# A graph layer with routed experts: identity transposes put ahead of TensorE's waits in the routing stage, behind the feed-forward and ahead of the experts' products

## The chip, the cores and the metric

The kernel runs on one core of one Trainium2 chip. A core has a matrix engine (TensorE, PE in the profile; its weight loads are listed as PEld), a vector engine (DVE), a scalar engine (ACT), GpSimd (POOL) and SyncE (SP). Each runs its own stream of instructions in order and waits for the others through semaphores. Sixteen DMA engines move data between the chip's memory and SBUF. The metric is the device time of one execution in microseconds, the median of the runs. The profile's rows show TensorE at one of two levels: the granted clock is 1.00 (2.4 GHz) or 0.50 (1.2 GHz).

## The reference

Everything is fp32. `x` has 6250 rows of 256. A graph attention layer (106250 edges) with batch normalisation comes first, its last part being a feed-forward of two 256x256 products over all nodes. Then each row is normalised, routed to the two best of eight experts, and the two experts' outputs are added to it:

```python
h = _batchnorm(x_attn + x, gamma1, beta1)
ffn = relu(h @ W1 + b1) @ W2 + b2
x = x + _batchnorm(ffn + h, gamma2, beta2)
z = _layernorm(x)
gate_scores = z @ Wg + bg                       # 6250 x 8
_, idx = top_k(gate_scores, 2)
h_e = gelu(z @ W1[e] + b1[e])                   # 256 -> 512, for the two chosen experts
y_e = h_e @ W2[e] + b2[e]                       # 512 -> 256
out = x + sum of y_e over the two chosen
```

## The kernel before

The program is a row of blocks with a barrier of all engines between them: preparing the edges, projecting the nodes, attention (the first two thirds of the time), joining the heads, the feed-forward, the routing, the experts, and a copy of the result. All of it is written out by hand, with semaphores. Three blocks are touched.

**Feed-forward** (`feed_forward`, L1367). The nodes go through in chunks of 250 columns. For each chunk TensorE does `up` (L1454) and `down` (L1463), eight instructions each. After the last `down` (L1475) TensorE has nothing left in this block, while VectorE finishes sums and the batch scale.

**Routing** (`route_tokens`, L1478). 6250 rows are 49 tiles of 128, in eight groups of 3, 5, 6, 7, 7, 7, 7, 7 tiles. For a tile t:

- ScalarE writes the batch-normalised features `y` (L1590, two per tile, semaphore `y_ready`), in a ring of three.
- TensorE turns them with two 128x128 transposes into `y_ps` (`turn_y`, L1639, semaphore `y_turned`).
- VectorE adds them to the rows of x (L1717, `summed`) and measures them (L1722). For a whole group it forms the row scale (`spread`, `inverse`), with a root on ScalarE.
- ScalarE writes the normalised rows `z` (L1607, `z_ready`); TensorE turns them with two transposes (`turn_z`, L1647); ScalarE copies them out of PSUM (L1597, `z_taken`); TensorE multiplies them with the 256x8 gate weights (`score`, L1660, four instructions of 8 columns, `scored`).
- VectorE chooses the experts of the group (12 small operations), TensorE counts ranks with four small matmuls (`ranks`, L1671 and L1672), VectorE turns ranks into places (11 small operations, the last one L1824), and GpSimd scatters each tile's rows twice, once for each chosen expert (L1892, indirect DMAs).

TensorE's order in group g is, for i = 0 to 7: `turn_y` of tile i of group g+1, `turn_z` of tile i of group g, `score` of tile i-1 of group g; `ranks` of group g-1 stands in the middle of the loop. VectorE interleaves `choose` and `places` of one group with the sums of a later one.

**Experts** (`apply_experts`, L1897). 56 slots of 256 rows. A slot has four transposes (`turn_z`, L1973), 16 instructions of `up` (L1982) and 16 of `down` (L1992). Ahead of the loop TensorE turns the biases (L1998), waits for the rows of slots 0 and 1 (`loaded`), turns them, and does `up(0)`; the loop begins with `up(1)`.

Of the kernel before, what the change touches and what calls it, by code (L numbers as in the profile page):

```python
# [16 lines left out]
P = 128  # L17
# [52 lines left out]
CHUNKS = N // W  # L70
# [48 lines left out]
def wait_past(engine, semaphore, value):  # L119

    if isinstance(value, int) and value <= 0:
        return
    engine.wait_ge(semaphore, value)
# [8 lines left out]

class Program:
    pass


def heads_of(row):
# [1229 lines left out]
def feed_forward(nc, k):  # L1367


    with ExitStack() as ctx:  # L1370
# [7 lines left out]
        up_ps = pb("f_up_ps", [P, 2, 2, 256])  # L1378
        down_ps = pb("f_down_ps", [P, 2, 2, 256])
        w_in = k.ffn_in  # L1380
        normed, up_done, hid_ready, down_done, summed, measured = (sem("f_normed"), sem("f_up"), sem("f_hid_s"), sem("f_down"),
                                                                   sem("f_summed"), sem("f_measured"))

        with nc.Block(no_gpsimd_drain=True) as block:
# [62 lines left out]
            @block.tensor  # L1447
            def _(pe):
                def up(c, s):
                    pe.wait_ge(normed, 2 * c + 2)  # L1450
                    wait_past(pe, hid_ready, 2 * c - 2)
                    for o in range(DH):
                        for h in range(DH):
                            last = nc.tensor.matmul(up_ps[:, s, o, 0:W], w1[:, h, o * P:(o + 1) * P],  # L1454
                                                    k.feat[:, h, bass.ds(c * W, W)], start=(h == 0), stop=(h == DH - 1))
                    last.then_inc(up_done, 1)

                def down(c, s):
                    pe.wait_ge(hid_ready, 2 * c + 2)
                    wait_past(pe, summed, 2 * c - 2)  # L1460
                    for o in range(DH):
                        for h in range(DH):
                            last = nc.tensor.matmul(down_ps[:, s, o, 0:W], w2[:, h, o * P:(o + 1) * P], hid[:, s, h],  # L1463
                                                    start=(h == 0), stop=(h == DH - 1))
                    last.then_inc(down_done, 1)

                pe.wait_ge(w_in, 96)
                up(0, 0)

                def both(c, s):  # L1470
                    up(c + 1, 1 - s)
                    down(c, s)

                tiles(pe, CHUNKS - 1, 2, 2, both)
                down(CHUNKS - 1, (CHUNKS - 1) % 2)  # L1475


def route_tokens(nc, k):  # L1478
# [6 lines left out]
    CHOICE, STEPS = 12, 22  # L1485
    half_of = lambda g: GROUPS[g] // 2
    Y_RING = 3
    tokens = lambda t: min(P, N - t * P)
    tiles_of = lambda g: range(FIRST[g], FIRST[g + 1]) if 0 <= g < len(GROUPS) else ()
    with ExitStack() as ctx:  # L1490
# [14 lines left out]

        y = spare((Y_RING, DH, P))
        zt = spare((2, DH, P))
# [33 lines left out]
        slot_f = sb("r_slot_f", [1, 2, SLOT_STEPS])  # L1541
        y_ps = pb("r_y_ps", [P, Y_RING, 512])
        zt_ps = pb("r_zt_ps", [P, 2, 512])
# [4 lines left out]
        y_ready, y_turned, summed, measured = sem("r_y_s"), sem("r_y_turned"), sem("r_summed"), sem("r_measured")  # L1548
        z_ready, z_turned, z_taken, scored = sem("r_z_s"), sem("r_z_turned"), sem("r_z_taken"), sem("r_scored")
# [4 lines left out]
        with nc.Block(no_gpsimd_drain=True) as block:  # L1554
# [30 lines left out]
            def _(act):  # L1585
                def norm(t):
                    n = tokens(t)
                    wait_past(act, y_turned, t - (Y_RING - 1))
                    for h in range(DH):
                        nc.scalar.activation(y[:, t % Y_RING, h, 0:n], k.feat[:, h, t * P:t * P + n], ACT.Identity,  # L1590
                                             scale=k.norm2[:, 0, h:h + 1], bias=k.norm2[:, 1, h:h + 1]).then_inc(y_ready, 1)
# [40 lines left out]
            @block.tensor  # L1632
            def _(pe):
                def turn_y(t):
                    n = tokens(t)
                    pe.wait_ge(y_ready, 2 * t + 2)
                    wait_past(pe, summed, t - (Y_RING - 1))
                    for h in range(DH):
                        last = nc.tensor.transpose(y_ps[0:n, t % Y_RING, h * P:(h + 1) * P], y[:, t % Y_RING, h, 0:n], k.ident[:, :])  # L1639
                    last.then_inc(y_turned, 1)  # L1640

                def turn_z(t):
                    n = tokens(t)
                    pe.wait_ge(z_ready, t + 1)
                    wait_past(pe, z_taken, t - 1)
                    for h in range(DH):
                        last = nc.tensor.transpose(zt_ps[:, t % 2, h * P:h * P + n], z[0:n, t, h * P:(h + 1) * P], k.ident[0:n, 0:n])  # L1647
                    last.then_inc(z_turned, 1)

                def biases(g):  # L1650

                    n = GROUPS[g]
                    nc.tensor.matmul(score_ps[:, g % 2, 0:n * E], ones[0:1, :], bg_all[:, 0:n, :].rearrange("o t e -> o (t e)"),
                                     start=True, stop=False, skip_group_check=True)

                def score(g, t):
                    n, i = tokens(t), t - FIRST[g]
                    pe.wait_ge(z_taken, t + 1)
                    for h in range(DH):
                        last = nc.tensor.matmul(score_ps[0:n, g % 2, i * E:(i + 1) * E], zt[:, t % 2, h, 0:n], wg[:, h, :],  # L1660
                                                start=False, stop=(h == DH - 1), skip_group_check=True)
                    last.then_inc(scored, 1)

                def ranks(g):
                    pe.wait_ge(routed, g * STEPS + CHOICE)
                    flat = either[:, :, :].rearrange("p t e -> p (t e)")
                    n = GROUPS[g]
                    whole = n if tokens(FIRST[g + 1] - 1) == P else n - 1
                    spans = [(0, whole, P)] + [(whole, n, tokens(FIRST[g] + whole))] * (whole < n)
                    for a, b, m in spans:  # L1670
                        nc.tensor.matmul(rank_ps[:, 0, a * E:b * E], below[0:m, :], flat[0:m, a * E:b * E], start=True, stop=True)  # L1671
                        last = nc.tensor.matmul(rank_ps[:, 1, a * E:b * E], ones[0:m, :], flat[0:m, a * E:b * E], start=True, stop=True)  # L1672
                    last.then_inc(ranked, 1)

                for t in tiles_of(0):
                    turn_y(t)
                pe.wait_ge(w_in, before_route + 32)
                pe.wait_ge(biased, 1)
                for g in range(len(GROUPS)):
                    biases(g)  # L1680
                    if g == 1:
                        ranks(0)
                    for i in range(G + 1):
                        if i < len(tiles_of(g + 1)):
                            turn_y(tiles_of(g + 1)[i])
                        if i < len(tiles_of(g)):
                            turn_z(tiles_of(g)[i])
                        if 1 <= i <= len(tiles_of(g)):
                            score(g, tiles_of(g)[i - 1])
                        if 2 <= g < LAST and i == half_of(g + 1):  # L1690
                            ranks(g - 1)
                ranks(LAST - 1)
                ranks(LAST)
# [203 lines left out]
def apply_experts(nc, k):  # L1897

    RING = 4
    with ExitStack() as ctx:  # L1900
# [21 lines left out]
        zt_ps = pb("x_zt_ps", [P, 2, DH, BATCH])  # L1922
        hid_ps = pb("x_hid_ps", [P, 2, HC, BATCH])
        y_ps = pb("x_y_ps", [P, 2, 2, D])
# [10 lines left out]
        with nc.Block(no_gpsimd_drain=True) as block:  # L1935
# [31 lines left out]
            def _(pe):  # L1967
                def turn_z(s, q):
                    pe.wait_ge(loaded[q % RING], (s - q % RING) * (32 // RING) + 32)
                    wait_past(pe, zt_ready, s - 1)  # L1970
                    for h in range(DH):
                        for u in range(2):
                            last = nc.tensor.transpose(zt_ps[:, q % 2, h, u * P:(u + 1) * P],  # L1973
                                                       z[:, q % RING, u, h * P:(h + 1) * P], k.ident[:, :])
                    last.then_inc(z_turned, 1)
# [11 lines left out]
                def down(s, q, e):  # L1987
                    pe.wait_ge(hid_ready, HC * s + HC)
                    wait_past(pe, y_ready, s - 1)
                    for u in range(2):  # L1990
                        for j in range(HC):
# [5 lines left out]
                pe.wait_ge(k.bias_in, 16 * (E + 1))  # L1997
                nc.tensor.transpose(y_ps[:, 0, 0, 0:E * HC], k.be1_rows[:, :],  # L1998
                                    k.ident[0:E * HC, 0:E * HC]).then_inc(bias_turned, 1)
                turn_z(0, 0)  # L2000
                turn_z(1, 1)
                pe.wait_ge(k.experts_in, 16 * E)
# [9 lines left out]
                n = SLOT_STEPS - 2  # L2012
# [77 lines left out]
def graph_ffn_kernel(nc, *args):  # L2090
# [23 lines left out]
    with ExitStack() as ctx:  # L2114
# [59 lines left out]
        with ExitStack() as layer:  # L2174
# [3 lines left out]
            join_heads(nc, k)  # L2178
            feed_forward(nc, k)
        route_tokens(nc, k)  # L2180
        apply_experts(nc, k)
        give_out(nc, k)
# [16 lines left out]
```

## Time and profile before

| | us |
|---|---|
| median of 3 runs | 2530.99 (2528.05 to 2534.24) |
| the profiled execution, its span | 2534.7 (the execution: 2536.48) |
| feed-forward, TensorE's part | about 1773 to 1861 |
| routing, TensorE's part | about 1867 to 2041 |
| wait for the last scatters and the barrier | about 2041 to 2079 |
| experts | about 2079 to the end |

Times inside the execution are counted from the start of the span. In a row of the profile "MATMUL a<-b,c x4" means four instructions on PE that write tile a; the time behind it reaches from the first's start to the last's end, or is the sum of busy time in a view of groups. A transpose on TensorE is listed as a MATMUL with `ident` among its inputs. Ends of matmuls are modelled.

### The profile page before, as it was taken

The numbers are of one execution on the slowest core, as the hardware profiler recorded it, in microseconds if no ns is written. First come the engines' busy times: TensorE is split into PE (matmuls) and PEld (weight loads), VectorE is DVE, ScalarE is ACT, GpSimd is POOL, SyncE is SP. The second block draws the span as 40 slices with busy tenths as digits, with TensorE's granted clock in tenths as the row PEclk, the third lists the DMA queues.
The fourth block names the chain that finished last, engine by engine and source line by source line (L and its number), as shares of the span: only waits on it lengthen the run. The fifth ranks groups of instructions, "written<-read, shape, count | busy, mean of one in ns | idle before, by whom it ended". The sixth has DMA issues, their size and how long they took to land. (4 is left out here: it accounts for less than half of the span.)

```text
span 2534.7 us, 43098 instructions
## 1 busy us (share of the span) xinstructions
PE 1952.2 (77%) x9344; PEld 1654.9 (65%) x9345; DVE 1530.2 (60%) x3518; ACT 1183.7 (47%) x2733; POOL 1364.5 (54%) x1263
## 2 busy tenths in 40 slices
PE   3974787888788878887888788853966519999994
PEld 2754676676676766776776667732855418888884
DVE  5955777777777777787777777889455311111110
ACT  3542555555555555555555555543545403223221
POOL 3346666666666666666666666538003543444442
PEclk9987998999899989998999899875975559999997
DMA  7676666666666666666666666533503345666665
GB/s 216 230 245 191 185 198 189 187 195 189 188 190 191 190 189 187 188 195 189 190 190 187 191 190 186 153 101 121 165 29 106 127 150 127 142 143 145 139 143 143
DMA packets 259360, 430.75 MB, mean 170 GB/s; under 512 B 46025, under 2 KB 130872, under 8 KB 259180
## 3 DMA queue, kind: packets, MB, share of 16 engines
q1 hardware_dynamic: 156320, 227.87, 28.1%
q0 software_dynamic: 66272, 154.09, 23.7%
q10 hardware_dynamic: 36716, 48.20, 6.1%
q8 instruction: 19, 0.31, 0.0%
q14 instruction: 33, 0.27, 0.0%
HBM read 365.32 MB, written 71.10 MB: 172 GB/s over the span
## 5 line engine op out<-in xcount | busy, mean ns | idle before, releaser
L820 POOL DMA_INDIRECT ring<-xl_rows,a_idx x928 | 956.1, 1030 | 514.6 <-issue 249.7
L1137 PE MATMUL a_f_ps<-a_xr_w,a_hot_n 128*128 128x256 f32 x1856 | 577.9, 393 | 59.2 <-ACT a_hot_n L884 31.1
L1139 PE MATMUL a_f_ps<-ring,ident 128*128 128x256 f32 x1856 | 584.1, 396 | 18.8 <-issue 18.7
L1150 PE MATMUL a_o_ps<-ring,a_hot_e 128*128 128x264 f32 x1856 | 532.6, 412 | 41.9 <-issue 21.0
L1137 PEld LDWEIGHTS a_f_ps<-a_xr_w,a_hot_n 128*128 128x128 f32 x1856 | 372.5, 202 | 132.9 <-issue 36.7
L1004 DVE SCALAR_TENSOR_TENSOR a_pos<-a_f_ps,att_cols 128x512 f32<-128x512 f32 x464 | 316.2, 681 | 224.9 <-remote 155.1
L1150 PEld LDWEIGHTS a_o_ps<-ring,a_hot_e 128*128 128x128 f32 x1856 | 367.0, 204 | 123.3 <-issue 43.9
L901 ACT ACTIVATE a_hot_e<-a_far_e,one 128x512 f32<-128x512 f32 x232 | 167.3, 721 | 352.4 <-PE a_o_ps L1150 168.8
L1014 DVE TENSOR_REDUCE a_lg<-a_pos 128x8 f32<-128x512 f32 x464 | 315.8, 681 | 15.3 <-remote 14.6
L1022 DVE TENSOR_TENSOR ring<-ring (+1 forms) x464 | 316.8, 683 | 7.3 <-ACT ring L929 3.9
L1139 PEld LDWEIGHTS a_f_ps<-ring,ident 128*128 128x128 f32 x1856 | 303.0, 200 | 26.0 <-issue 25.9
L1959 POOL DMA_INDIRECT acc_rows<-ring,x_idx x112 | 175.3, 1566 | 261.0 <-DVE ring L2057 133.5
L894 ACT ACTIVATE a_far_e<-iota_row,a_near_rel 128x128 f32<-128x128 f32 x928 | 294.8, 388 | 1.6 <-issue 0.3
L1034 DVE TENSOR_TENSOR acc<-a_o_ps,acc 128x264 f32 x464 | 197.3, 425 | 125.5 <-PE a_o_ps L1150 59.0
L884 ACT ACTIVATE a_hot_n<-a_far_n,one 128x512 fp32r<-128x512 f32 x232 | 167.5, 722 | 190.7 <-remote 117.2
L2056 DVE CAST x_idx<-ring 128x2 int32<-128x2 f32 x56 | 9.5, 170 | 408.7 <-PE x_y_ps L1992 408.7
L1982 PE MATMUL x_hid_ps<-ring,x_w 128*128 128x256 f32 x896 | 204.5, 382 | 0.0
L1992 PE MATMUL x_y_ps<-we,ring 128*128 x896 | 202.5, 379 | 0.0
L1982 PEld LDWEIGHTS x_hid_ps<-ring,x_w 128*128 128x128 f32 x896 | 171.8, 192 | 23.7
L1992 PEld LDWEIGHTS x_y_ps<-we,ring 128*128 128x128 f32 x896 | 166.0, 190 | 20.3
L878 ACT ACTIVATE a_far_n<-a_rel_bc,neg_col 128x512 f32<-128x512 bf16 x232 | 164.9, 711 | 22.7 <-issue 19.5
L1892 POOL DMA_INDIRECT disp_rows<-r_z,r_idx x98 | 96.7, 987 | 109.7 <-DVE r_idx L1824 82.3
(323 smaller groups left out, 2050.1 us busy)
## 6 DMA issues: line engine op xcount, KB each, us to landing
a_xr_w<-xr_rows SPq DMA_DIRECT2D x464, 256.0 KB
a_rel_bc<-rel_rows ACTq DMA_DIRECT2D x116, 256.0 KB
x_w<-in_L_ffn_W_dram SPq DMA_DIRECT2D x56, 512.0 KB
ring<-xl_rows,a_idx POOLq DMA_INDIRECT x928
ring<-disp_rows SPq DMA_DIRECT2D x56, 257.0 KB
xr_rows<-xr_parts SPq DMA_DIRECT2D x50, 256.0 KB, 2.0
xl_rows<-xl_sb SPq DMA_DIRECT2D x50, 132.0 KB, 1.8
j_xl<-xl_rows SPq DMA_DIRECT2D x25, 264.0 KB, 2.8
```

Source lines behind the costliest of these rows:

```text
L820: nc.gpsimd.indirect_dma_start(xl_e[:, p * T + 2 * h + u, :], None, k.xl_rows, bass.IndirectOffsetOnAxis(ap=idx[:, p, 2 * h + u:2 * h + u ...
L894: nc.scalar.activation(far_e[:, u, :], k.iota_row[:, :], ACT.Abs, bias=near_rel[:, j * QT + u:j * QT + u + 1]).then_inc(far_e_ready, 1)
L1004: nc.vector.scalar_tensor_tensor(pos[:, h % 2], f_ps[:, h % FS], 0.0, att, ALU.max, ALU.mult).then_inc(settled, 1)
L1014: nc.vector.tensor_reduce(lg[:, :, 2 * h:2 * h + 2].rearrange("p h t -> p t h"), pos[:, h % 2].rearrange("p t (h c) -> p t h c", c=C), AX. ...
L1022: nc.vector.tensor_tensor(at[:, :, :, 0:C], at[:, :, :, 0:C], at[:, :, :, C:C + 1].to_broadcast([P, 2, H, C]), ALU.mult).then_inc(msg_read ...
L1034: nc.vector.tensor_tensor(at, o_ps[:, o_slot(hh), 0:XW], at, ALU.add).then_inc(added, 1)
L1137: nc.tensor.matmul(f_ps[:, h % FS, u, :], hot_n[:, j % 2, 2 * g + u, :], xr_w[:, h % XR, a, :].bitcast(F32R), start=(a == 0), stop=False)
L1139: last = nc.tensor.matmul(in_heads(f_ps[:, h % FS, u, :]), k.ident[:, :], heads_of(xl_e[:, p * T + 2 * h + u, :])[:, :, 0:C], start=False, ...
L1150: last = nc.tensor.matmul(o_ps[:, o_slot(hh), 0:XW], hot_e[:, j % 2, 2 * g + u, :], xl_e[:, pp * T + 2 * hh + u, :], start=(u == 0), stop= ...
L1959: nc.gpsimd.indirect_dma_start(k.acc_rows, bass.IndirectOffsetOnAxis(ap=idx[:, q, u:u + 1], axis=0), y[:, q, u], None, compute_op=ALU.add) ...
L1982: last = nc.tensor.matmul(hid_ps[:, q % 2, j], w1[:, q % RING, h, j * P:(j + 1) * P], zt[:, q % 2, h], start=(h == 0), stop=(h == DH - 1))
L1992: last = nc.tensor.matmul(y_ps[:, q % 2, u], hid[:, q % 2, j, u * P:(u + 1) * P], k.we2[:, bass.ds(e, 1), j, :].rearrange("p o n -> p (o n)"),
```

## The change

A helper is added that issues n transposes of the 128x128 identity into a given piece of PSUM. No instruction reads what they write, and they raise no semaphore.

```diff
+def keep_warm(nc, k, out, n):
+    for _ in range(n):
+        nc.tensor.transpose(out, k.ident[:, :], k.ident[:, :])
...
                 tiles(pe, CHUNKS - 1, 2, 2, both)
                 down(CHUNKS - 1, (CHUNKS - 1) % 2)
+                keep_warm(nc, k, up_ps[:, CHUNKS % 2, 0, 0:P], 50)
...
+    FILL = 4
...
                 def turn_y(t):
                     n = tokens(t)
+                    wait_past(pe, summed, t - (Y_RING - 1))
+                    keep_warm(nc, k, y_ps[:, t % Y_RING, 0:P], FILL)
                     pe.wait_ge(y_ready, 2 * t + 2)
-                    wait_past(pe, summed, t - (Y_RING - 1))
...
                 def turn_z(t):
                     n = tokens(t)
+                    wait_past(pe, z_taken, t - 1)
+                    keep_warm(nc, k, zt_ps[:, t % 2, 0:P], FILL)
                     pe.wait_ge(z_ready, t + 1)
-                    wait_past(pe, z_taken, t - 1)
...
                 nc.tensor.transpose(y_ps[:, 0, 0, 0:E * HC], k.be1_rows[:, :],
                                     k.ident[0:E * HC, 0:E * HC]).then_inc(bias_turned, 1)
+                keep_warm(nc, k, hid_ps[:, 0, 0, 0:P], 36)
                 turn_z(0, 0)
```

So there are 50 transposes behind the feed-forward's last product, 2 x 4 for each of the 49 tiles of the routing (392), and 36 ahead of the experts' first rows. In the rows of the changed kernel the helper is L141; other lines of these blocks move down by 7 to 11.

On TensorE, at the border of the feed-forward and the routing. Before:

```order
L1463 MATMUL f_down_ps<-f_hid,f_w 128x250 [waits f_summed,f_hid_s]
L1463 MATMUL f_down_ps<-f_hid,f_w 128x250 x3
L1384 UNCONDITIONAL_BRANCH
L1632 UNCONDITIONAL_BRANCH [waits barrier_Pool_Activation_PE_DVE_SP_release]
L1639 MATMUL r_y_ps<-ident,ring 128x128 [waits r_y_s]
L1639 MATMUL r_y_ps<-ident,ring 128x128
```

And changed:

```order
L1470 MATMUL f_down_ps<-f_hid,f_w 128x250 [waits f_summed,f_hid_s]
L1470 MATMUL f_down_ps<-f_hid,f_w 128x250 x3
L141 MATMUL f_up_ps<-ident 128x128 x50
L1391 UNCONDITIONAL_BRANCH
L1641 UNCONDITIONAL_BRANCH [waits barrier_Pool_Activation_PE_DVE_SP_release]
L141 MATMUL r_y_ps<-ident 128x128 x4
L1649 MATMUL r_y_ps<-ident,ring 128x128 [waits r_y_s]
L1649 MATMUL r_y_ps<-ident,ring 128x128
```

The 50 stand ahead of the barrier, so TensorE reaches it after them; the first four of the routing stand behind it, ahead of the wait for `y` (the semaphore of tile `y` is called r_y_s here).

On TensorE, one tile in the middle of a routing group (a tile of the next group turned, one of this group turned, one scored). Before:

```order
L1639 MATMUL r_y_ps<-ident,ring 128x128 [waits r_summed,r_y_s]
L1639 MATMUL r_y_ps<-ident,ring 128x128
L1647 MATMUL r_zt_ps<-ident,r_z 128x128 [waits r_z_taken,r_z_s]
L1647 MATMUL r_zt_ps<-ident,r_z 128x128
L1660 MATMUL r_score_ps<-r_wg,ring 128x8 [waits r_z_taken]
L1660 MATMUL r_score_ps<-r_wg,ring 128x8
```

And changed:

```order
L141 MATMUL r_y_ps<-ident 128x128 [waits r_summed]
L141 MATMUL r_y_ps<-ident 128x128 x3
L1649 MATMUL r_y_ps<-ident,ring 128x128 [waits r_y_s]
L1649 MATMUL r_y_ps<-ident,ring 128x128
L141 MATMUL r_zt_ps<-ident 128x128 [waits r_z_taken]
L141 MATMUL r_zt_ps<-ident 128x128 x3
L1658 MATMUL r_zt_ps<-ident,r_z 128x128 [waits r_z_s]
L1658 MATMUL r_zt_ps<-ident,r_z 128x128
L1671 MATMUL r_score_ps<-r_wg,ring 128x8 [waits r_z_taken]
L1671 MATMUL r_score_ps<-r_wg,ring 128x8
```

The wait for a free buffer now stands alone, ahead of the four; the wait for the data stands behind them. Nothing stands ahead of the wait of a score. (A score of one tile is four instructions on the chip, two of these rows with two each.)

On TensorE, at the start of the experts. Before:

```order
L1998 MATMUL x_y_ps<-ident,be_rows 128x32 [waits bias_in]
L1973 MATMUL x_zt_ps<-ident,ring 128x128 [waits x_loaded0]
L1973 MATMUL x_zt_ps<-ident,ring 128x128 x3
L1973 MATMUL x_zt_ps<-ident,ring 128x128 [waits x_loaded1]
L1973 MATMUL x_zt_ps<-ident,ring 128x128 x3
L1982 MATMUL x_hid_ps<-ring,x_w 128x256 [waits x_zt,experts_in]
```

And changed:

```order
L2009 MATMUL x_y_ps<-ident,be_rows 128x32 [waits bias_in]
L141 MATMUL x_hid_ps<-ident 128x128 x36
L1984 MATMUL x_zt_ps<-ident,ring 128x128 [waits x_loaded0]
L1984 MATMUL x_zt_ps<-ident,ring 128x128 x3
L1984 MATMUL x_zt_ps<-ident,ring 128x128 [waits x_loaded1]
L1984 MATMUL x_zt_ps<-ident,ring 128x128 x3
L1993 MATMUL x_hid_ps<-ring,x_w 128x256 [waits x_zt,experts_in]
```

The 36 stand between the biases and the wait for the first slot's rows. The other engines' streams are the same but for line numbers.

## Rows read from the trace of the kernel before

**Rows 1.** The page: span, and the clock granted in 40 equal slices.
```profile
span 2534.7 us, 43098 instructions
...
PEclk9987998999899989998999899875975559999997
```

**Rows 2.** Stretches: us, PE busy (x instructions), granted clock, DMA share, GB/s.
```profile
1773.00:1861.00 88.00, 87.59 (x400) 0.96 0.38 121
1861.00:1867.00 6.00, 0.00 (x0) 0.79 0.00 0
1867.00:2041.00 174.00, 104.77 (x444) 0.50 0.29 99
2098.00:2500.00 402.00, 402.00 (x1971) 1.00 0.61 136
```

**Rows 3.** Groups of PE's instructions, 1866 to 2045: busy, mean ns | idle before, releasers.
```profile
L1660 PE MATMUL r_score_ps<-r_wg,ring 128*128 128x8 f32 (+1 forms) x196 | 45.4, 345 | 34.2 <-ACT ring L1597 27.6 <-issue 6.3
L1639 PE MATMUL r_y_ps<-ident,ring 128*128 128x128 f32 (+1 forms) x98 | 32.6, 436 | 19.1 <-ACT ring L1590 19.0
L1647 PE MATMUL r_zt_ps<-ident,r_z 128*128 128x128 f32 (+1 forms) x98 | 31.9, 431 | 12.7 <-ACT r_z L1607 8.0 <-issue 3.2 <-DVE acc L1717 0.6
```

**Rows 4.** PE in order of time: start, us, instructions, [idle before <-releaser].
```profile
1773.22 6.55 PE L1454 MATMUL f_up_ps<-ring,f_w 128*128 128x250 f32 x16 [6.96 <-ACT ring L1425]
...
1891.10 0.69 PE L1647 MATMUL r_zt_ps<-ident,r_z 128*128 128x128 f32 x2 [4.96 <-ACT r_z L1607]
...
2079.38 0.28 PE L1998 MATMUL x_y_ps<-ident,be_rows 32*128 32x32 f32 x1 [38.44 <-PEq L1554]
...
2087.87 1.12 PE L1973 MATMUL x_zt_ps<-ident,ring 128*128 128x128 f32 x4 [1.65 <-DMA ring<-disp_rows]
2088.78 9.26 PE L1982 MATMUL x_hid_ps<-ring,x_w 128*128 128x256 f32 x32
2097.87 0.60 PE L1973 MATMUL x_zt_ps<-ident,ring 128*128 128x128 f32 x4
```

**Rows 5.** PE in order of time, two tiles of group 2: scores follow one another.
```profile
1908.32 0.86 PE L1660 MATMUL r_score_ps<-r_wg,ring 128*128 128x8 f32 x4
...
1909.92 0.86 PE L1660 MATMUL r_score_ps<-r_wg,ring 128*128 128x8 f32 x4
```

**Rows 6.** One stretch of group 2: us, PE busy, granted clock.
```profile
1908.00:1912.00 4.00, 4.00 (x22) 0.50 0.00 0
```

**Rows 7.** A wait of PE in group 3, in order of time.
```profile
1955.12 1.02 PE L1660 MATMUL r_score_ps<-r_wg,ring 128*128 128x8 f32 x4 [5.75 <-ACT ring L1597]
```

**Rows 8.** GpSimd's scatters as a group, then GpSimd and DVE in order of time.
```profile
L1892 POOL DMA_INDIRECT disp_rows<-r_z,r_idx x98 | 96.7, 987 | 109.7 <-DVE r_idx L1824 82.3 <-issue 27.4
...
1977.03 0.97 POOL L1892 DMA_INDIRECT disp_rows<-r_z,r_idx  x1 [0.30 <-issue]
1985.52 0.96 POOL L1892 DMA_INDIRECT disp_rows<-r_z,r_idx  x1 [7.52 <-DVE r_idx L1824]
...
1980.40 0.22 DVE L1797 COPY r_total<-r_rank_ps 128x56 f32<-128x56 f32 x1 [5.63 <-remote]
```

**Rows 9.** Stretches where the clock changes: us, PE busy, granted clock.
```profile
1862.00:1864.00 2.00, 0.00 (x0) 1.00 0.00 0
1864.00:1866.00 2.00, 0.00 (x0) 0.63 0.00 0
...
1778.00:1780.00 2.00, 2.00 (x8) 0.71 1.10 347
...
2092.00:2094.00 2.00, 2.00 (x8) 0.70 0.00 0
```

**Rows 10.** DVE's last operation of the feed-forward, ACT's first of the routing.
```profile
1865.96 0.16 DVE L1199 TENSOR_TENSOR norm<-f_par,f_tmp 128x2 f32<-128x2 f32 x1
...
1866.67 1.65 ACT L1590 ACTIVATE ring<-ring,norm 128x128 f32<-128x128 f32 x4 [1.94 <-PEq L1384]
```

## The prediction, made before the changed kernel ran

> **What bounds the kernel now.** I first read the slices of the page [rows 1]: the granted clock is near full everywhere but in the joining of the heads and in the routing. The table of stretches [rows 2] puts numbers on it. In the routing (1867 to 2041) TensorE is at 0.50 throughout; in the experts (from 2098 on) it is busy all the time at 1.00. So a microsecond won ahead of the experts is won at the end, and one lost is lost, since TensorE has no idle time there to give back.
>
> Then I asked what ends last inside the routing. It is not one engine. The groups of TensorE's instructions [rows 3] show 19.1 us of idle time ahead of `turn_y` (ScalarE's y is late), 12.7 ahead of `turn_z` and 34.2 ahead of the scores. In the early groups, where nothing else interferes, TensorE works without a gap [rows 6] and a tile takes 1909.92 - 1908.32 = 1.60 us [rows 5]: there TensorE sets the pace, with ScalarE and VectorE close to it. In the four later full-length passes (groups 2 to 5) there is another loop: GpSimd scatters a group (one DMA every 1.27 us), and while it does, TensorE's semaphores arrive late, so that all engines stand still for some 5 us (TensorE 5.75 us [rows 7], VectorE 5.63 us for the ranks [rows 8]). The ranks come only after the scatters' end (1977.03 + 0.97 = 1978.0; VectorE takes them at 1980.40), then VectorE needs until about 1985.5 for the places, and the next scatters start at 1985.52 [rows 8]. In this loop TensorE's speed counts only between 1980.4 and 1985.5: three tiles at 1.60 us.
>
> **The price of a transpose.** At half clock four take 1.12 us and two take 0.69 [rows 4], so one more costs (1.12 - 0.69) / 2 = 0.215 us; at full clock half of that, 0.107 (four: 0.60 [rows 4]). A tile of the routing gets eight more: +1.72 us at half clock, so 1.60 becomes 3.32; at full clock old and new work together take 3.32 / 2 = 1.66. All 392 cost 84.3 us of TensorE at half clock, 42.1 at full. The waits behind them hide at most 19.1 + 12.7 = 31.8 us [rows 3]; the 34.2 ahead of the scores have no transposes ahead of them. So the question is the clock, not the number.
>
> **When the clock moves.** It falls 3.5 us after TensorE has stopped: nothing runs from 1861, and the share 0.63 between 1864 and 1866 puts the fall at 1864.5 [rows 2, 9]. It rises after 5.9 us (1773.22 to 1779.2) and 4.4 us (2088.8 to 2093.2) of products back to back [rows 4, 9]. But in 1908 to 1912 TensorE was busy without a gap and the clock stayed at 0.50 [rows 6]. There half of the instructions are scores with 8 columns and half are transposes. The trace has no long stretch of transposes alone, so it doesn't show whether they raise the clock. With the change 12 of a tile's 16 instructions are transposes of 128 columns. I take it that they do count, since they stream the same columns through the array as a product does and follow one another at the same pace at either level; nothing in the trace says so directly.
>
> The Trainium skill says otherwise: "TensorE: Matmul & The Clock Gate", Part 4 (PE-mode transpose), states that the full clock does not engage for transposes, as they don't count as busy in the same way. By that rule the change would only add work. The same place gives 390 ns alone and 275 ns inside a kernel for one transpose.
>
> **Part 1, behind the feed-forward.** At full clock 50 x 0.107 = 5.3 us from 1860.9 on, to 1866.2. VectorE ends its part at 1866.1 and ScalarE starts the routing at 1866.67 [rows 10]; the cover is just long enough: 0 to +0.4, I take +0.2. If the clock falls at 1864.5 all the same, 34 are done and 16 x 0.215 = 3.4 us remain, to 1867.9: +1.7.
>
> **Part 2, the routing.** The clock starts high, but in groups 0 and 1 TensorE waits 4.96 us at a time for z [rows 4], with only four or eight transposes ahead of the wait, so it falls. From then on each working stretch starts at half clock and rises after 4.4 to 5.9 us: 1.3 to 1.8 tiles at 3.32 instead of 1.60, +2.3 to +3.1, say +2.7. For the stretch at 1891 all of this is on the path: +2.7. After each of the four standstills in the later passes it is so too, but the transposes ahead of the first turns have run during the standstill; I take half, 4 x 1.35 = +5.4 (bounds 0 and 4 x 3.1 = 12.4). At the high level a turn and a score end sooner (four transposes 1.12 against 0.60 [rows 4], so two win about 0.25 and a score about 0.4), which shortens the way from the row scale to the first score and the ranks: about -0.65 in five groups, -3.2 (bounds 0 and -6.5). Sum of the routing: +2.7 + 5.4 - 3.2 = +4.9, bounds -4 and +15. The buffer waits that now come first are on the same semaphores as before, and nothing else is queued behind them than what was: 0.
>
> **Part 3, ahead of the experts.** The biases are turned at 2079.4 to 2079.7; the rows of slot 1 arrive at 2087.87 [rows 4]. 36 transposes take 36 x 0.215 = 7.7 us at half clock, to 2087.4, inside that wait. If the clock rises meanwhile they end near 2086, and the 1.9 us to 2087.87 are shorter than the 3.5 us after which it fell. Then `up` of slots 0 and 1 runs at full clock: now the 4.6 us up to 2093.2 are at half, so -2.3, and -0.2 for the turn of slot 1: -2.5. If nothing rises: 2087.4 + 1.1 for slot 0's turn pushes slot 1's back: 0 to +0.7.
>
> **Sum.** 0.2 + 4.9 - 2.5 = +2.6 on an execution of 2536.5 (span 2534.7 and 1.8 around it). The median is 5.5 lower, so 2531.0 + 2.6, rounded to 2534.
>
> **Rivals.**
>
> A. Transposes don't raise the clock. Then every tile costs 3.32 where TensorE sets the pace. In the early stretches (1891 to 1900, 1903 to 1916) that is 5 + 6 tiles: 11 x 1.72 = +18.9. In each of four later passes 0 to 3 tiles stand on the path between the late semaphores and the next scatters; I take 1.8, as part of the work still runs in the standstill: 4 x 1.8 x 1.72 = +12.4. Bounds 19 and 40, sum +31. With +1.7 and +0.4 of the other parts: +33, 2564. For it: at 1908 to 1912 a gapless mix with transposes stayed low [rows 6]. Against it: there were as many short instructions in it. The rule of the Trainium skill above would give this.
>
> B. They do count, and the clock hardly falls in the routing at all, because the four ahead of each turn bridge the waits. Then 1.66 against 1.60 us costs nothing that the waits don't hide, and the shorter ways win 8 x 0.8 = -6; with -2.5: -8.5, 2522. For it: most waits are under 3.5 us. Against it: those of 5 us.
>
> C. They count, but with scores between them the mix is too thin to raise the clock in most stretches (slower, one mechanism): the early 11 tiles mostly at 3.32, +15, the later passes +7, the ends -2.5: about +20, 2551. It decides from the point where a tile's four scores keep the clock from rising.
>
> **How the numbers follow.** Likeliest case 47% (own range 2525 to 2543), A 25% (2552 to 2573), B 18% (2516 to 2526), C 10%. What a measurement can tell from no change is 0.2%, 5 us. Faster by more: B and the low end of the likeliest (0.07): 0.25. Within: most of the likeliest, 0.28. Slower by more: A, C and the high end (0.12): 0.47. The range that leaves out 2 in 10 cuts half of B and the upper end of A: 2522 to 2568.
>
> **What would show it.** The granted clock from 1867 on: 0.50 throughout means A; 1.00 throughout means B; a change of level in each group means the forecast, and with it a TensorE that after each standstill takes 3.3 us for the first tile and 1.7 for the third. In the experts the clock should be high by 2088, and the 32 instructions of the first two `up` take 7 us instead of 9.26. The prediction is wrong if the standstills of about 5 us themselves change, which I left as they are, or if other engines than I assume set the pace of the early tiles.

## The result and the profile after

The changed kernel takes 2550.43 us (median of four runs, 2547.33 to 2552.35) against 2530.82 (2528.05 to 2534.24): the ratio is 1.007, 95% interval 1.0056 to 1.0084. That is +19.6 us where the likeliest case said +2.6. The range held it, but by luck: it was wide because it also covered rivals A and B, and the case that I called likeliest (2525 to 2543) did not hold the time. The profiled execution has a span of 2547.5 us, 12.8 more than before; the two executions stand 5.7 above and 1.1 below their medians, so the traces show some 7 us less than the medians do.

First the page of the changed kernel, then three stretches of it (columns: us, busy time and instructions of PE, PEld, DVE, ACT and POOL, granted clock, DMA share, GB/s).

```profile
span 2547.5 us, 43961 instructions
...
PEclk9987988999899989998898989865987759999997
```

```profile
1776.00:1864.00 88.00, 87.56 (x440) 78.96 (x439) 41.01 (x112) 40.62 (x92) 0.18 (x1) 1.00 0.32 100
1864.00:2057.00 193.00, 129.32 (x836) 121.03 (x834) 89.19 (x399) 80.75 (x204) 73.55 (x76) 0.74 0.27 90
...
2110.00:2500.00 390.00, 390.00 (x1913) 343.57 (x1912) 42.95 (x106) 114.93 (x266) 165.44 (x106) 1.00 0.63 139
```

The routing (second stretch) now has a mean clock of 0.74 where [rows 2] had 0.50: about half of it runs at full clock. The stretch is also 19 us longer as cut here; from its first to its last mark the routing grew by 16.8 (table below). In the experts nothing has changed but the beginning. The groups of TensorE's instructions in the routing:

```profile
L141 PE MATMUL r_zt_ps<-ident 128*128 128x128 f32 x196 | 38.4, 332 | 0.0
L141 PE MATMUL r_y_ps<-ident 128*128 128x128 f32 x196 | 37.3, 322 | 0.4 <-PEq L1391 0.4
L1671 PE MATMUL r_score_ps<-r_wg,ring 128*128 128x8 f32 (+1 forms) x196 | 32.6, 276 | 33.8 <-ACT ring L1606 31.1 <-issue 2.2
L1658 PE MATMUL r_zt_ps<-ident,r_z 128*128 128x128 f32 (+1 forms) x98 | 24.6, 342 | 7.3 <-ACT r_z L1616 3.8 <-issue 3.3
L1649 PE MATMUL r_y_ps<-ident,ring 128*128 128x128 f32 (+1 forms) x98 | 22.5, 317 | 10.8 <-ACT ring L1599 10.8
```

Against [rows 3] the waits ahead of `turn_y` and `turn_z` shrank from 19.1 and 12.7 us to 10.8 and 7.3, so the added transposes filled a part of them. The 34.2 us ahead of the scores, where the long waits are, stayed (33.8). The clock goes up and down, here while groups 0 and 1 are scored:

```profile
1872.00:1875.00 3.00, 3.00 (x16) 3.00 (x16) 0.76 (x2) 3.00 (x9) 0.00 (x0) 0.50 0.03 5
1876.00:1881.00 5.00, 2.90 (x27) 2.61 (x24) 3.54 (x14) 1.94 (x5) 0.00 (x0) 1.00 0.21 72
1882.00:1891.00 9.00, 5.55 (x25) 5.15 (x26) 4.81 (x27) 3.17 (x9) 3.50 (x4) 0.50 0.12 41
1893.00:1902.00 9.00, 6.97 (x61) 6.42 (x60) 5.25 (x22) 3.57 (x10) 0.97 (x1) 1.00 0.31 109
```

**Where the time went.** The clearest mark is the start of VectorE's last operation of a group's places (`CAST r_idx`), after which GpSimd can scatter the group. I call the time between two of them a pass and use it for every kernel below. The last row of the table counts from ScalarE's first `y` of the routing to the last group's places.

| us | before | after | e2 | e5 | e6 | e7 | e8 |
|---|---|---|---|---|---|---|---|
| places of group 0 to 1 | 28.6 | 30.1 | 31.3 | 29.3 | 31.1 | 31.3 | 38.7 |
| 1 to 2 | 20.1 | 24.5 | 25.0 | 22.4 | 21.1 | 20.7 | 27.8 |
| 2 to 3 | 22.9 | 26.6 | 27.3 | 24.6 | 24.0 | 23.5 | 30.0 |
| 3 to 4 | 25.1 | 27.7 | 27.7 | 26.6 | 25.1 | 25.2 | 34.9 |
| 4 to 5 | 25.1 | 27.5 | 27.5 | 26.7 | 25.1 | 25.1 | 34.3 |
| 5 to 6 | 25.8 | 27.2 | 28.7 | 28.6 | 25.8 | 25.8 | 32.5 |
| whole | 176.8 | 193.6 | 197.2 | 188.7 | 181.4 | 181.8 | 231.7 |

The routing is 16.8 us longer, and every pass takes part. The four passes from 1 to 2 up to 4 to 5 each hold one standstill ahead of the places that end them; the first pass holds none, and in the last one (5 to 6) no `ranks` stands in the middle of TensorE's loop. (The kernels e1, e3 and e4, whose routing does the same work as before, give 175.2 to 176.2, so such a sum repeats within 1.6 us.)

**Inside a later pass.** TensorE in group 4, first in the kernel before:

```profile
1969.74 0.65 PE L1671 MATMUL r_rank_ps<-r_either,r_below 128*128 128x56 f32 x2
...
1970.62 0.65 PE L1639 MATMUL r_y_ps<-ident,ring 128*128 128x128 f32 x2
...
1976.54 1.02 PE L1660 MATMUL r_score_ps<-r_wg,ring 128*128 128x8 f32 x4 [4.85 <-ACT ring L1597]
...
1980.91 1.03 PE L1660 MATMUL r_score_ps<-r_wg,ring 128*128 128x8 f32 x4 [2.40 <-ACT ring L1597]
```

and in the changed kernel:

```profile
1976.68 0.60 PE L141 MATMUL r_zt_ps<-ident 128*128 128x128 f32 x4
1977.11 0.38 PE L1658 MATMUL r_zt_ps<-ident,r_z 128*128 128x128 f32 x2
1985.44 1.02 PE L1671 MATMUL r_score_ps<-r_wg,ring 128*128 128x8 f32 x4 [7.94 <-ACT ring L1606]
1986.31 0.66 PE L1682 MATMUL r_rank_ps<-r_either,r_below 128*128 128x56 f32 x2
...
1987.18 1.07 PE L141 MATMUL r_y_ps<-ident 128*128 128x128 f32 x4
```

Before, `ranks` and one more tile of y are through when the standstill begins; only the message is late (VectorE takes the ranks at 1980.40 [rows 8]). Now the standstill catches TensorE one tile sooner, with `ranks` still to be done. It isn't much longer: before, TensorE waits 4.85 us, gets one tile further and waits 2.40 more, 7.25 together; now it waits 7.94 at once. What VectorE and GpSimd make of it (for a wait marked `<-remote` the profile names no engine):

```profile
1987.92 0.42 DVE L1728 TENSOR_TENSOR acc<-r_y_ps,acc 128x256 f32<-128x256 f32 x1 [7.00 <-remote]
...
1988.60 0.20 DVE L1808 COPY r_total<-r_rank_ps 128x56 f32<-128x56 f32 x1
...
1991.67 0.42 DVE L1728 TENSOR_TENSOR acc<-r_y_ps,acc 128x256 f32<-128x256 f32 x1 [1.26 <-PE r_y_ps L1649]
...
1995.52 0.97 POOL L1903 DMA_INDIRECT disp_rows<-r_z,r_idx  x1 [10.11 <-DVE r_idx L1835]
```

From the end of the standstill to the next scatter it is 1995.52 - 1987.92 = 7.6 us, where [rows 8] give 1985.52 - 1980.40 = 5.1: VectorE has one more addition to do ahead of the ranks, and then waits for a `turn_y` behind transposes. This is the +2.5 of such a pass.

The pass from group 1 to 2 has the same standstill and loses in the same way. VectorE before, then in the changed kernel:

```profile
1931.06 0.42 DVE L1717 TENSOR_TENSOR acc<-r_y_ps,acc 128x256 f32<-128x256 f32 x1 [5.16 <-remote]
...
1931.90 0.21 DVE L1797 COPY r_total<-r_rank_ps 128x48 f32<-128x48 f32 x1
```

```profile
1931.07 0.42 DVE L1728 TENSOR_TENSOR acc<-r_y_ps,acc 128x256 f32<-128x256 f32 x1 [2.85 <-remote]
...
1933.35 0.21 DVE L1808 COPY r_total<-r_rank_ps 128x48 f32<-128x48 f32 x1 [1.51 <-PE r_rank_ps L1683]
```

The ranks lay ready before; now VectorE waits for TensorE to compute them. From the end of VectorE's last late wait to the places it takes 1940.19 - 1931.07 = 9.1 us against 1936.57 - 1931.06 = 5.5. For groups 3, 4 and 5 the same time is 8.4, 6.6 and 6.4 us against 4.6, 4.1 and 4.1. These four together are +12.2 of the 16.8 us.

**The experts' beginning** in the changed kernel, in order of time, and under it two stretches in which TensorE runs nothing but the added transposes:

```profile
2093.91 5.60 PE L141 MATMUL x_hid_ps<-ident 128*128 128x128 f32 x36
2099.41 0.66 PE L1984 MATMUL x_zt_ps<-ident,ring 128*128 128x128 f32 x4
2101.95 0.66 PE L1984 MATMUL x_zt_ps<-ident,ring 128*128 128x128 f32 x4 [1.88 <-DMA ring<-disp_rows]
2102.44 7.07 PE L1993 MATMUL x_hid_ps<-ring,x_w 128*128 128x256 f32 x32
```

```profile
2094.00:2096.00 2.00, 2.00 (x10) 2.00 (x11) 0.00 (x0) 0.19 (x1) 0.00 (x0) 0.50 0.00 0
2097.00:2099.00 2.00, 2.00 (x20) 2.00 (x19) 0.00 (x0) 0.00 (x0) 0.00 (x0) 1.00 1.00 347
```

The clock rises while only identity transposes run, 10 instructions in 2 us become 20, and the first two `up` take 7.07 us where [rows 4] had 9.26. The DMA share goes from 0.00 to 1.00 between the two stretches as well, but the clock doesn't need that: in [rows 9] it is 0.70, on its way up, in 2092 to 2094 with a DMA share of 0.00.

### The profile page after: what moved, and what is told of

Its sections match the earlier page's. It is cut to its first block and busy times, and to the rows that moved or that the text cites. A ratio compares the mean times of both kernels' runs of the same rounds, so it can differ in the third digit from the quotient of the medians.

```text
span 2547.5 us, 43961 instructions
## 1 busy us (share of the span) xinstructions
PE 1993.6 (78%) x9822; PEld 1702.5 (67%) x9823; DVE 1529.8 (60%) x3518; ACT 1187.2 (47%) x2733; POOL 1368.5 (54%) x1263
## 5 line engine op out<-in xcount | busy, mean ns | idle before, releaser
L1144 PE MATMUL a_f_ps<-a_xr_w,a_hot_n 128*128 128x256 f32 x1856 | 581.3, 395 | 59.7 <-ACT a_hot_n L891 30.1
```

Source lines behind the costliest of these rows:

```text
L1144: nc.tensor.matmul(f_ps[:, h % FS, u, :], hot_n[:, j % 2, 2 * g + u, :], xr_w[:, h % XR, a, :].bitcast(F32R), start=(a == 0), stop=False)
```

## The experiments

The first eight ran on chips where the kernel before takes what it took above (2532.0 and 2532.6 us); the last four on a chip where it takes 2263.1 us, which matters below. Their lines move by up to 11 against the kernel before.

**e1: the 36 ahead of the experts alone.**

```diff
+                keep_warm(nc, k, hid_ps[:, 0, 0, 0:P], 36)
                 turn_z(0, 0)
```

> The kernel before with the 36 transposes ahead of the experts' rows and nothing else. Theory: they hide behind the wait for the rows of slot 1 and raise the clock before `up` of slot 0. In the changed kernel the stretch from the bias turn to the end was 453.8 us against 455.3, so -1.5 us (2529.3), and the granted clock reads 1.00 when `up` of slot 0 starts. Rival: identity transposes by themselves don't raise the clock, and in the changed kernel it was high for another reason: then 0 to +0.7 us, and 32 instructions of `up` take 9.3 us as before.

Measured: ratio 0.9998 (0.9986 to 1.0009), so nothing that the medians can tell. In the trace the stretch from the bias turn to the end takes 453.0 us against 455.3: -2.3 (expected -1.5). The clock is 0.50 in a stretch 0.3 to 2.3 us after the bias turn and 1.00 from 3.3 us on, with only transposes in both. The rival on the clock is refuted.

**e2: the eight per tile of the routing alone.**

```diff
+    FILL = 4
...
+                    wait_past(pe, summed, t - (Y_RING - 1))
+                    keep_warm(nc, k, y_ps[:, t % Y_RING, 0:P], FILL)
                     pe.wait_ge(y_ready, 2 * t + 2)
```

> The kernel before with the eight transposes per tile in the routing alone (four ahead of each turn); none behind the feed-forward, none ahead of the experts. Theory: the whole loss sits here, since the places of the last group came 16.8 us later in the changed kernel: +17 to +21 us (2548 to 2552), and the places of the groups come at the times of the changed kernel, within 1 us. Rival: part of the loss needs the 50 behind the feed-forward, whose high clock the first tiles of the routing inherit: then the first groups differ by more than 2 us from the changed kernel.

Measured: 2550.88 us, ratio 1.0077 (1.0058 to 1.0096): all of the loss, as expected. The passes are those of the changed kernel within 1.5 us, the whole is 3.6 longer. The first pass differs (31.3 against 30.1), so the high clock that the 50 hand over may be worth a microsecond or so there; one execution of each doesn't prove it.

**e3: the 50 behind the feed-forward alone; e4: the new order of the waits with no transposes** (`FILL = 0`).

> The kernel before with the 50 transposes behind the feed-forward's last product alone. Theory: they end before VectorE's last operation of that block, and the clock that they hold high falls again in the first waits of the routing: 0 us (within 1). Rival 1: they delay the barrier: +1 to +2. Rival 2: the first turns and scores at the high clock shorten the way to the first scatters: -1 to -2.

> The routing with the waits in the new order (the free buffer first, then the data) and no transposes added anywhere. Theory: both waits must be over before the turn in either order, so 0 us (within 1). Rival: a wait that now stands as an instruction of its own costs TensorE's queue something on each of 98 turns: at 0.06 us each +6 us, and the time of a tile where TensorE sets the pace rises from 1.60 to 1.7 us or more.

Measured: e3 0.9999 (0.9983 to 1.0016), e4 0.9991 (0.9982 to 1.0000), wholes of 175.8 and 175.2 us. Both parts are free, as forecast.

**e5 and e6: which transposes of a later pass cost.** e5 leaves out those of the three tiles behind `ranks` in groups 2 to 6, e6 has only those.

```diff
                     for i in range(G + 1):
+                        fill = 0 if 2 <= g < LAST and i > half_of(g + 1) else FILL
```

> The routing's transposes alone, as in e2_routing, but none for the three tiles behind `ranks` in groups 2 to 6 (120 of 392 left out). In the changed kernel a later pass takes 27.7 us against 25.1, and 6.8 us lie between the end of the standstill and the places of the group, against 4.3 before. Theory: the fill-up at half clock of exactly these three tiles is what a pass loses; without it a pass takes 25.1 to 25.4 us and only the early groups' loss stays: +7 to +10 us (2539 to 2542). Rival: the loss of a pass is in the standstill or in what stands ahead of it (VectorE is one addition further back when it begins): then a pass still takes 26.5 us or more, and the time stays above +14.

> The complement of e5_spare: transposes only for the three tiles behind `ranks` in groups 2 to 6 (120), none elsewhere. The clock stays at 0.50 nearly everywhere, since each such stretch starts low. Theory: all of a pass's loss is here, +2.5 us in each of the four later passes and somewhat more, as without the fill-up ahead the clock never rises earlier: +10 to +16 us in all, a pass of 27.7 to 29 us, groups 0 to 2 as before. Rival: below +6, passes below 26.5.

Measured: e5 1.0051 (1.0032 to 1.0070), 2545.0 us, and e6 1.0020 (1.0003 to 1.0036), 2536.9 us; the medians are 12.4 and 4.3 above the kernel before, where I had expected +7 to +10 and +10 to +16. My theory of that moment falls: the passes of e6 from 3 to 4 on are 25.1 and 25.8 as before, though its tiles behind `ranks` carry eight transposes at half clock; those of e5 are still 26.6 and more. VectorE in e6, then in e5:

```profile
2005.47 0.22 DVE L1808 COPY r_total<-r_rank_ps 128x56 f32<-128x56 f32 x1 [6.34 <-remote]
...
2009.64 0.18 DVE L1835 CAST r_idx<-r_place 128x14 int32<-128x14 f32 x1
```

```profile
2007.80 0.42 DVE L1728 TENSOR_TENSOR acc<-r_y_ps,acc 128x256 f32<-128x256 f32 x1 [6.98 <-remote]
...
2008.70 0.22 DVE L1808 COPY r_total<-r_rank_ps 128x56 f32<-128x56 f32 x1
...
2013.48 0.18 DVE L1835 CAST r_idx<-r_place 128x14 int32<-128x14 f32 x1
```

In e6 the ranks come first and the places 4.2 us later; in e5 an addition comes first and it takes 5.7. So in the passes from 3 to 5 the transposes ahead of the standstill lose the tile, and those behind add their own price (27.6 less 26.6) only once it is lost. e6 also shows that behind `ranks` they do cost in the first three passes: +2.5, +1.0 and +1.1 us.

**e7: one transpose ahead of each turn; e8: eight** (`FILL = 1`, `FILL = 8`).

> The routing's transposes alone, one ahead of each turn in place of four (98). One tile of TensorE then takes 1.60 + 2 x 0.215 = 2.03 us at half clock, 1.0 at full. Theory: with so few the clock stays at 0.50 as before and each tile on the path pays 0.43 us: some 11 early tiles and 2 to 3 in each of four passes, +8 (2540), bounds +5 and +9. Rival: one is enough to keep the clock up through the waits of 1 to 3 us, and the routing gets no slower: 0 to -4, with the clock at 1.00 for more than half of the routing.

> The routing's transposes alone, eight ahead of each turn in place of four (784). A tile of TensorE takes 1.60 + 16 x 0.215 = 5.04 us at half clock, 2.5 at full. Theory: the clock rises after each standstill as it does with four, so the first tile costs 5.04 and the others 2.5, 0.9 more than before: early groups about +15, each later pass 5.04 + 2 x 2.5 against 3 x 1.60, about +5: +33 to +38 in all (2566). Rival: eight bridge the standstills (16 x 0.107 = 1.7 us of work in a wait of 5) so that the clock never falls: then 2.5 against 1.60 per tile on the path, +0.9 x 20 = +18 or less.

Measured: e7 1.0024 (1.0007 to 1.0042), e8 1.0204 (1.0175 to 1.0232), 2586.0 us. e7's median is 6.7 above the kernel before, inside the +5 to +9 expected, but not where I had put it. With one the clock stays low (a mean of 0.51), and yet the passes 3 to 4 and 4 to 5 are 25.2 and 25.1: TensorE still gets through `ranks` ahead of the standstill. The first three passes pay 2.7, 0.6 and 0.6. With eight the last three passes lose 7 to 10 us, not 5. So the pass from 3 to 4 doesn't lose in proportion: 0 with one, 2.6 with four, 9.8 with eight. My size for e8 (+33 to +38, measured +53) was too small; in its trace 13.9 us lie between VectorE's last late wait and the places of group 4, against 6.6 with four and 4.1 before, so more work is left for after the standstill than I had counted.

**e9 and e10: scatters held back, without and with the transposes.** GpSimd waits for the places of all groups before its first scatter.

```diff
-                    pool.wait_ge(rows_ready, g + 1)
+                    pool.wait_ge(rows_ready, len(GROUPS))
```

> The kernel before, with GpSimd holding back every scatter until the places of all groups are known; no transposes added. Both theories of the standstill meet here. Theory: TensorE's semaphores are late only while GpSimd scatters, so the standstills vanish and a later pass takes 13 to 17 us (seven tiles at 1.60 and the waits at the group's border) against 25.1; the 98 scatters then follow in one row of about 125 us, so the whole is 50 to 80 us slower. Rival: the semaphores are late for a reason of their own (the engines' order, the copy of x): then a pass stays at 20 us or more.

> e9_held with the routing's 8 transposes per tile. It measures what they cost where TensorE isn't disturbed. Theory: short waits let the clock stay at 1.00 for most of it, a tile takes 1.66 against 1.60 and only the stretch after each fall is dear: +1 to +2.5 us per pass, +7 to +15 over the eight groups against e9_held. Rival: the clock alternates as in the changed kernel and a tile costs 2.3 us or more on average: +5 us per pass, +25 or more. Second rival: the later passes' loss of 2.6 us comes from the standstill alone, and here it is zero.

Measured, one execution each: 2357.5 and 2362.9 us (before: 2263.1). e9 is 94 slower, more than the 50 to 80 expected, and its passes are 16.2 us. But that says nothing on the scatters: on this chip e12, which scatters in each pass, has passes of 16.2 too. Its VectorE and GpSimd in group 4:

```profile
1734.31 0.97 POOL L1900 DMA_INDIRECT disp_rows<-r_z,r_idx  x1 [0.30 <-issue]
...
1735.39 0.22 DVE L1805 COPY r_total<-r_rank_ps 128x56 f32<-128x56 f32 x1 [1.26 <-PE r_rank_ps L1680]
...
1735.59 0.97 POOL L1900 DMA_INDIRECT disp_rows<-r_z,r_idx  x1 [0.31 <-issue]
```

The ranks reach VectorE after a wait of 1.26 us while GpSimd scatters at the same pace of 1.28 us as everywhere. There is no standstill on this chip, with or without scatters, so scatters alone don't make TensorE's semaphores late.

What e9 and e10 do tell is the price without a standstill: passes of 16.8, 16.9, 16.0 and 16.0 us against 16.2, then 20.6 against 15.9, and 146.3 against 138.6 in all: +7.7, at the low end of the +7 to +15 expected (one trace of each; the two spans differ by 5.3). The clock is 0.82 on average there. A tile in e10 where all is dense, and two of the last full group, where only `turn_z` and scores are left:

```profile
1655.71 0.51 PE L1670 MATMUL r_score_ps<-r_wg,ring 128*128 128x8 f32 x4
...
1657.42 0.51 PE L1670 MATMUL r_score_ps<-r_wg,ring 128*128 128x8 f32 x4
...
1756.24 0.86 PE L1670 MATMUL r_score_ps<-r_wg,ring 128*128 128x8 f32 x4
...
1758.26 0.86 PE L1670 MATMUL r_score_ps<-r_wg,ring 128*128 128x8 f32 x4
```

1.71 us per tile at full clock against 1.60 without transposes at half clock [rows 5]: nearly nothing, as worked out (1.66). At half clock four transposes make a tile without y take 2.02 us, where e9 has 1.17 (1751.96 - 1750.79, the starts of two scores), and most of the +7.7 is there: the clock is 0.50 from 1750 to 1762.

**e11: 20 transposes as a delay.** Four ahead of the third `turn_y` of the groups 2 to 6, none elsewhere.

```diff
-                            turn_y(tiles_of(g + 1)[i])
+                            turn_y(tiles_of(g + 1)[i], 4 if 2 <= g < LAST and i == 2 else 0)
```

> The kernel before with only four transposes in each of the groups 2 to 6, ahead of the third turn of y (20 in all). They push TensorE back by 0.86 us at the point where, in the kernel before, its third tile of y is added by VectorE 7.8 us after the places, the last one before the semaphores stop coming. Theory (in place of my first one, which e5_spare and e6_behind contradict): what a pass loses is one tile that no longer gets through ahead of the standstill, so 20 transposes cost nearly what 272 did in e5_spare: a pass of 26.6 us against 25.1, +5 to +7 us in all. Rival: the loss is in proportion to TensorE's added work: 0.86 us per pass at most, a pass of 25.1 to 26.0.

Measured: 1.0007 (0.9998 to 1.0017), passes of 15.6 to 17.1 us. It fell on the chip without standstills, where it can only show the plain price: against e12 the pass from 3 to 4 is 0.9 longer for 0.86 us of delay, others 0.9 longer to 0.6 shorter, and the whole is +2.6. Whether 20 transposes would cost a pass its tile where there is a standstill stays untested.

**e12: transposes only in two long waits.**

```diff
-                            turn_z(tiles_of(g)[i])
+                            turn_z(tiles_of(g)[i], 22 if g == 1 and i == 0 else 0)
...
+                keep_warm(nc, k, hid_ps[:, 0, 0, 0:P], 36)
```

> A candidate: transposes only where TensorE waits long and nothing of its own is delayed: 22 ahead of the first turn of z in group 1 (22 x 0.215 = 4.7 us in a wait of 4.96) and 36 ahead of the experts' rows; nothing elsewhere. Theory: the experts' part gives -1.5 to -2.3 as in e1_experts, and group 1's stretch at full clock gives 0 to -1.5, ScalarE and VectorE being close behind TensorE there: -2 to -3.5 us (2528.5), too little to be told from no change for certain. Rival: the 22 outlast the wait because the clock doesn't rise in time, +0.5, and the stretch gains nothing: -1.5 in all.

Measured: 2259.8 us, ratio 0.9987 (0.9978 to 0.9996): -3 us, the only kernel here that is faster than the kernel before beyond its interval, if by little. Of it the experts give 2.4 (452.8 us from the bias turn to the end against 455.2 in e11). The 22 give nothing: the pass takes 28.5 us, as in e9 without them. Three stretches of e12 around them, then the scores of its whole routing:

```profile
1646.00:1650.00 4.00, 3.79 (x18) 3.38 (x16) 3.19 (x20) 0.80 (x3) 1.75 (x2) 0.50 0.09 33
1651.00:1653.00 2.00, 1.06 (x8) 0.85 (x9) 0.62 (x2) 2.00 (x6) 1.51 (x2) 1.00 0.29 103
1654.00:1656.00 2.00, 2.00 (x11) 2.00 (x11) 0.57 (x3) 1.97 (x6) 1.07 (x2) 0.50 0.26 88
```

```profile
L1668 PE MATMUL r_score_ps<-r_wg,ring 128*128 128x8 f32 (+1 forms) x196 | 43.1, 334 | 2.7 <-ACT ring L1604 2.7
```

The clock is up when the tiles come, TensorE is then busy only 1.06 of 2 us while ScalarE is busy 2.00, and soon the clock is down again. At full clock ScalarE is the bound of these tiles. The last row is the other side of the standstill: here the scores wait 2.7 us in all, on the other chip 34.2 [rows 3].

## Why the prediction was right and wrong, point by point

- **Does the clock rise for transposes?** Right, and it was the doubtful point. Identity transposes alone raise it (rows of the experts' beginning). Rival A falls with it. The rule of the Trainium skill that I weighed ("TensorE: Matmul & The Clock Gate", Part 4, PE-mode transpose) says that it doesn't; the trace disagrees (20 instructions in 2 us after 10 in 2 us), unless the page means a mode that these fp32 transposes don't use, which no row shows. The page's 275 ns inside a kernel is for a bf16 transpose and can't be set against the steps from one fp32 transpose to the next here, 0.215 us at half clock and 0.107 at full.
- **Part 1, the 50:** +0.2 forecast, e3 shows none. The clock is 1.00 to 1864 in the changed kernel.
- **Part 3, the experts:** -2.5 forecast, -1.5 in the changed kernel's trace and -2.3 and -2.4 in e1 and e12.
- **Part 2, the routing, is the step that failed:** +4.9 forecast, +16.8 measured (its upper bound was +15). By the starts of `CAST r_idx` it splits in three. (1) Up to the places of group 1, without a standstill: +2.7 forecast, +2.0 measured. (2) The four passes with a standstill, groups 1 to 5: +5.4 forecast, with bounds 0 and 12.4; they take 106.4 us against 93.1, +13.3. This is the term that was mis-sized. I let TensorE's speed count only behind each standstill and costed half of a first tile there. The groups' traces, e5 and e6 show that the transposes ahead of it decide, by leaving `ranks` for after it. (3) The last pass, for which the forecast had nothing: +1.4, with its cause not tested. The fourth term, the shorter ways at the high level (-3.2), has no passes of its own, and where it should show it doesn't: the turns and scores at a group's start are where the clock is low. From the first turn of z to the first score of group 2 it takes 1905.99 - 1903.12 = 2.87 us against 1906.56 - 1904.27 = 2.29, changed kernel first:

```profile
1903.12 0.69 PE L1658 MATMUL r_zt_ps<-ident,r_z 128*128 128x128 f32 x2 [0.17 <-ACT r_z L1616]
...
1905.99 0.51 PE L1671 MATMUL r_score_ps<-r_wg,ring 128*128 128x8 f32 x4
```

```profile
1904.27 0.69 PE L1647 MATMUL r_zt_ps<-ident,r_z 128*128 128x128 f32 x2 [0.57 <-ACT r_z L1607]
...
1906.56 1.02 PE L1660 MATMUL r_score_ps<-r_wg,ring 128*128 128x8 f32 x4 [0.33 <-ACT ring L1597]
```

  Together 7.9 + 1.4 + 3.2 - 0.7 = 11.8 of the 11.9 us that the sum was short.
- **"Wrong if the standstills themselves change":** half of this happened. In group 4 their end didn't move (VectorE goes on 2.4 us after the last scatter in [rows 8] and 2.5 after it in the changed kernel) and TensorE's waits there hardly grew (7.25 to 7.94 us), but their beginning catches less finished work.
- **Rival C** gave 2551, the time that was measured, with a clock that is mostly low. The time fits by chance: the clock was high for half of the routing, and the passes with a standstill lose for another reason. **Rival B** is refuted in the changed kernel (mean clock 0.74), yet e10 comes near to it where nothing stands still: 0.82, and two passes 0.2 shorter than without transposes.
- The routing and the experts account for 16.8 - 1.5 = 15.3 us; the spans show 12.8, mostly because the routing of the changed kernel's execution starts 2.9 us sooner, and the medians show 19.6. These differences are within what single executions differ by, and I can't assign them.

**What stays open:** why TensorE's semaphores come late on the chips of the first eight experiments and of the comparison itself, and not on that of the last four. It isn't the scatters alone (e12), and e9 can't say whether they are needed. That losing `ranks` is what costs such a pass is read from the traces, e5 and e6; e11, which was to test it by itself, fell on the chip without standstills. The changed kernel was not run on the chip of the last four. An estimate from e10 and e12: there GpSimd's scatters bind from about the fourth group on (its last places are known at 139.0 us, its last scatter starts at 171.7), so that only the 3.4 us by which e10's fourth group is later than e12's (85.5 against 82.1) would count, less 2.4 for the experts: about +1.

## What to carry to other kernels

Filling TensorE's waits paid where one long wait stands right ahead of dense products that bind the end, as ahead of the experts: 36 transposes bought 2.3 us in the trace of e1, too little for its medians to show. It didn't pay in this pipeline of short operations with waits of 1 to 5 us: the clock fell in the waits at the groups' borders, so the filling was paid at half clock just where each group begins, and in e12 the high clock came when ScalarE was the bound. And where a recurring standstill cuts a loop, ask which step just gets through ahead of it: work that seems to fit in idle time can push that step behind it.

## What the runs showed of the hardware that I had not expected

- TensorE's full clock is granted to identity transposes alone: 0.50 then 1.00, with 10 and 20 of them in 2 us.
- A stretch of turns and 8-column scores lost the full clock that 22 transposes had given it (1.00, then 0.50 at 1654 in e12); with eight transposes per tile it kept it within a group (1.00 from 1893 to 1902 in the changed kernel).
- The same kernel takes 2531 us on some chips and 2263 on another. In the routing the difference is the standstills (passes of 25.1 against the 16.2 us of e12, whose routing has only 22 transposes more, with scatters at the same 1.28 us), and the part ahead of it is 240 us shorter too (the routing begins at 1626 instead of 1867).
